# A graph layer on one core: edge tiles of 128 rows in place of 125, another order of SyncE's queue ahead of the mixer, one-hot rows made by pairs

## The reference, cut to what matters

```
xn = layernorm(x)
el, er = (xn W_src + b) . attn_l,  (xn W_dst + b) . attn_r      # 8 heads per node
e      = leaky_relu(el[src] + er[dst]);  a = softmax of e over the edges of one dst
gnn    = segment_sum(feat_v[src] * a, dst)                      # feat_v = xn W_val + b
mix    = linear attention over all nodes (random features of xn Wq, xn Wk; then Wo)
x1     = x + gnn + mix
out    = x1 + expert FFN (8 experts, Sinkhorn gates, top-k rows routed) of layernorm(x1)
```

## Time and profile before

| | us |
|---|---|
| median of 3 runs | 3210.87 (3203.05 to 3212.89) |
| the profiled execution | 3184.74 |
| its span | 3182.6 |
| busy: PE, POOL, DVE, ACT | 2569.4, 2209.5, 1621.1, 993.6 |
| mean granted TensorE clock | 0.907 of full |

### The profile page before, as it was taken

How to read it: one execution, slowest core, us unless ns; L and a number is a source line. 1 busy time by engine, 2 the same in 40 slices (tenths; PEclk the granted TensorE clock), 3 DMA queues, 4 the chain that set the end, 5 groups by cost and what they waited for, 6 DMA issues and landing times.

```text
span 3182.6 us, 47522 instructions
## 1 busy us (share of the span) xinstructions
PE 2569.4 (81%) x10463; PEld 1790.9 (56%) x10464; DVE 1621.1 (51%) x2963; ACT 993.6 (31%) x2564; POOL 2209.5 (69%) x1847
## 2 busy tenths in 40 slices
PE   6689999999999989951676777777888988934998
PEld 3366677776677744420454556665666766723443
DVE  6612222222222269985854555555666666767232
ACT  2312222222222210020454444554555655600111
POOL 6287778777778777877877877777777777600454
PEclk9889999999999989985699998898988999955999
DMA  4341121111111133420566667777777777630111
GB/s 144 122 105 33 31 37 29 29 29 29 30 31 29 23 105 119 117 64 3 157 174 173 176 181 183 185 186 182 194 193 187 196 193 195 175 111 0 45 52 38
DMA packets 276032, 341.23 MB, mean 107 GB/s; under 512 B 164855, under 2 KB 184030, under 8 KB 275850
## 3 DMA queue, kind: packets, MB, share of 16 engines
q0 software_dynamic: 218672, 227.51, 31.6%
q1 hardware_dynamic: 51709, 93.57, 9.1%
q10 hardware_dynamic: 5594, 19.52, 1.7%
HBM read 285.65 MB, written 55.25 MB: 107 GB/s over the span
## 4 chain that ended last, share of the span: by engine, by line
POOL 41%; PE 19%; issue 16%; DMA 13%; DVE 8%; DVEq 2%; POOLq 0%; ACT 0%; ACTq 0%
POOL R L552 31%; PE ps L640 17%; DMA R<-val_tab,src_i 11%; POOL R L594 8%; POOL er_starts L565 2%; DMA work<-in_x_dram 1%; DVEq L239 1%; DVE R L1463 1%; DVE work L1557 1%; DMA R<-in_L_gnn_b_dst_dram 1%; PE ps L934 1%; DVEq L1463 1%; PE ps L664 1%; DVE R L1444 0%; DVE R L1500 0%
## 5 line engine op out<-in xcount | busy, mean ns | idle before, releaser
L640 PE MATMUL ps<-R,work 125*125 (+3 forms) x5240 | 1650.6, 470 | 225.7 <-DVE R L1463 207.2
L640 PEld LDWEIGHTS ps<-R,work 125*125 125x125 f32 (+2 forms) x5240 | 987.6, 195 | 795.0 <-issue 655.7
L552 POOL DMA_INDIRECT R<-el_tab,src_i x800 | 984.6, 1231 | 341.1 <-issue 288.7
L594 POOL DMA_INDIRECT R<-val_tab,src_i x800 | 978.7, 1223 | 280.7 <-issue 180.8
L1463 DVE TENSOR_TENSOR R<-R,ps (+1 forms) x800 | 521.2, 693 | 131.4 <-DVE ps L1452 125.6
L1113 ACT ACTIVATE work<-work 125x125 f32<-125x125 f32 x900 | 277.8, 309 | 500.0 <-PE ps L640 472.1
L640 PE MATMUL ps<-work,R 128*128 128x250 f32 x1600 | 359.5, 383 | 21.8 <-DMA work<-R 21.8
L1110 ACT ACTIVATE work<-work,negdst 125x125 f32<-125x125 f32 x900 | 353.6, 393 | 59.2 <-issue 34.5
L640 PEld LDWEIGHTS ps<-work,R 128*128 128x128 f32 x1600 | 308.9, 194 | 59.1 <-issue 21.8
L1452 DVE COPY ps<-R (+1 forms) x401 | 69.9, 175 | 299.2 <-POOLq L600 227.1
L1295 DVE TENSOR_TENSOR R<-ps,R 125x512 f32<-125x512 f32 x50 | 34.6, 692 | 358.1 <-PE ps L640 358.1
(11 more groups left out here) (256 smaller groups left out, 2186.0 us busy)
## 6 DMA issues: line engine op xcount, KB each, us to landing
work<-in_x_dram SPq DMA_DIRECT2D x33, 500.0 KB
R<-el_tab,src_i POOLq DMA_INDIRECT x800
R<-val_tab,src_i POOLq DMA_INDIRECT x800, 5.9
val_tab<-R SPq DMA_DIRECT2D x50, 253.9 KB
work<-R SPq DMA_DIRECT2D x25, 500.0 KB
work<-xm_tab SPq DMA_DIRECT2D x50, 250.0 KB
out_dram<-R SPq DMA_DIRECT2D x50, 250.0 KB
xm_tab<-work ACTq DMA_DIRECT2D x17, 500.0 KB
```

The costliest lines, as they stand in the source:

```text
L552: eng.indirect_dma_start(out=ELP[:, g, c, :], out_offset=None, in_=el_tab[:, :], in_offset=bass.IndirectOffsetOnAxis(ap=src_i[:, t:t + 1], ...
L594: eng.indirect_dma_start(out=ring[:, slot, :], out_offset=None, in_=val_tab[:, :], in_offset=bass.IndirectOffsetOnAxis(ap=src_i[:, 2 * u + ...
L640: return pe.matmul(o, l, r, start=start, stop=stop)
```

## The change

**Edge tiles.** An edge tile has B = 128 rows. The edges are laid out as 16 chunks of CT = 49 tiles (NT = 784 places), of which NE = 782 hold edges; CL is 6272, and the 13 blocks have 512 columns, the last one 128. `src` and `dst` come from the host as before, 125 to a column. `src` is therefore turned on the chip: ACT loads it, DVE casts it, PE turns it (7 products), DVE copies it (3), SP writes it to DRAM (3 DMAs) and reads it back as 112 rows of 896, PE turns these (7 products), DVE copies them to `src_i` (2). `dst` is loaded as 112 rows of 896, negated by DVE, turned by PE (7 products) and copied by DVE (2), all between mixer and output. The zero fill of `er_starts` and its reading back have 128 rows of partitions in place of 125.

```
+B = 128
+CT = -(-E // (NCH * B))
+CL = CT * B
+NT = NCH * CT
+EQ = NT * B
+NE = -(-E // B)
...
-            for u in range(ET // 2):
+            for u in range(NE // 2):
                 eng.wait_ge(S["tile_free"], 2 * u + 2)
                 gather_pair(u)
...
+            eng.wait_ge(S["consts_ready"], 2)
+            eng.wait_ge(S["edge_rows"], 4)
+            n_ = (NI - 1) * 128 * P
+            eng.dma_start(src_nat[0:n_].rearrange("(j p n) -> p j n", p=128, n=P), src_turned[:, 0:NI - 1, :]).then_inc(S["idx_loaded"], 16)
...
+            eng.wait_ge(S["idx_loaded"], 64)
+            eng.dma_start(src_rows, src_nat.rearrange("(p n) -> p n", p=NR)).then_inc(S["idx_loaded"], 16)
...
+            st.done(v.memset(negdst_rows[lo:NR, REST:NI * B], -NOBODY))
+            st.done(v.tensor_scalar(negdst_rows[lo:NR, 0:REST], dst_i[lo:NR, 0:REST], -1.0, None, ALU.mult))
+            v.tensor_scalar(negdst_rows[0:NR - 1, :], dst_i[0:NR - 1, :], -1.0, None, ALU.mult).then_inc(S["edge_rows"], 1)
+            v.wait_ge(S["edge_psum"], 3)
```

```
             def load_x(g):
                 if g >= NXI:
-                    if g % 2:
-                        return
                     eng.wait_ge(S["xn_transposed"], g - NXI + 1)
...
+                    if g == G - NXI:
+                        load_weights()
```

```
-                for s in range(2):
-                    k2 = 2 * (u + c) + s
-                    fn(absd[s][0:P, :], iota_f[0:P, :], ACT.Abs, bias=negdst[:, bass.ds(2 * u + s, 1)]).then_inc(S["act_step"], 1)
-                    act.wait_ge(S["act_step"], k2 + c + 1)
-                    act.wait_ge(S["onehot_free"], k2 + 1)
+                fn(absd[0], row_of(c), ACT.Abs, bias=negdst[:, bass.ds(2 * u, 1)])
+                fn(absd[1], row_of(c), ACT.Abs, bias=negdst[:, bass.ds(2 * u + 1, 1)]).then_inc(S["act_step"], 1)
+                act.wait_ge(S["act_step"], (u + c) + 1 + shifts)
+                for s in range(2):
+                    act.wait_ge(S["onehot_free"], 2 * (u + c) + s + 1)
```

More of the change, by code:

```diff
@@ L65, in block_tiles @@
 def block_tiles(k):
-    return NCH * (min(TB * k + TB, CT) - TB * k)
+    return sum(c * CT + g < NE for g in range(TB * k, min(TB * k + TB, CT)) for c in range(NCH))
 def logits_by(k):
@@ L385, in store_el, with load_weights @@
                 eng.dma_start(el_v[:, 2 * g:2 * g + 2, :], elr_all[:, 0, 2 * g:2 * g + 2, :]).then_inc(S["el_written"], 16)
[L387 to L396, removed]
+            def load_weights():
                 eng.wait_ge(S["welr_ready"], 1)
@@ L519, in _ @@
             eng.sem_inc(S["consts_ready"], 1)
-            for t_ in (ident[:, :], halves[:, :], half2[:, :], before[:, :], EW2[:, ET // 2, :]):
+            for t_ in (ident[:, :], halves[:, :], half2[:, :], before[:, :]):
                 st.done(eng.memset(t_, 0.0))
@@ L606, in _ @@
                     report(u - BEHIND)
-            for u in range(ET // 2 - BEHIND, ET // 2):
+            for u in range(NE // 2 - BEHIND, NE // 2):
                 report(u)
@@ L998, in trip @@
                     copy_xT(g, b % 2)
-                    if more and b % 2:
-                        load_x(g + NXI, b)
                     if not isinstance(g, int) or g >= 1:
@@ L1237, in fold_logit_weights @@
                 v.wait_ge(S["elr_params"], 96)
-                v.wait_ge(S["rows_spread"], 1)
-                s_al, s_ar, s_bs, s_bd = [ps[:, 4 + r, :] for r in range(4)]
                 for w_, a_, o_ in ((s_wsrc, s_al, 0), (s_wdst, s_ar, H)):
@@ L1387, in _, with columns @@
             v.wait_ge(S["er_t_copied"], NB)
-            def columns(k):
-                return TB * k * P, min(TB * k * P + TB * P, CL)
-            for k in range(NB):
-                lo, hi = columns(k)
-                st.done(v.tensor_tensor_scan(out=scan_x[:, lo:hi], data0=scan_p[:, lo:hi], data1=scan_m[:, lo:hi],
-                                             initial=0.0 if k == 0 else scan_x[:, lo - 1:lo], op0=ALU.mult, op1=ALU.add))
-                st.done(v.tensor_scalar(scan_p[:, lo:hi], scan_p[:, lo:hi], -1.0, -FAR, ALU.add, ALU.mult))
-                st.done(v.tensor_scalar(scan_d[:, lo:hi], scan_d[:, lo:hi], ends[:, 2:3], FAR, ALU.subtract, ALU.mult))
+            st.done(v.tensor_tensor_scan(out=scan_x, data0=scan_p[:, 0:CL], data1=scan_m, initial=0.0, op0=ALU.mult, op1=ALU.add))
+            st.done(v.tensor_scalar(scan_p[:, 0:CL], scan_p[:, 0:CL], -1.0, -FAR, ALU.add, ALU.mult))
             st.done(v.memset(scan_p[:, CL:CL + 1], FAR))
             st.done(v.memset(scan_p[:, 0:1], 0.0))
+            st.done(v.tensor_scalar(scan_d, scan_d, ends[:, 2:3], FAR, ALU.subtract, ALU.mult))
+            def columns(k):
+                return TB * k * B, min(TB * k * B + TB * B, CL)
             for i, k in enumerate(range(NB - 1, -1, -1)):
```

247 lines of the change are left out of this document (150 added, 97 removed).

## The result

The changed kernel takes 4207.88 us in the median of 4 runs (4195.51 to 4217.59), the kernel before 3209.64 (3203.05 to 3212.89): a ratio of 1.3111, with an interval of 1.307 to 1.3153. The forecast was 3015. The profiled execution took 4217.59 us (span 4215.5), against 3184.74 (3182.6) before: 1032.9 us more.

What follows compares the result with a forecast made beforehand. The prediction took the number of POOL's gathers and the price of one to bound the kernel. Its terms, -8 + 1 - 8 - 37 - 144 = -196 us, off a median of 3211 gave 3015 us, range 2955 to 3070.

Steps and rivals of the forecast that it cites:

- The price of a gather: POOL's logit and value gathers: 128 rows cost 1.02 us, with 0.30 between 1.32 us, where 125 rows took 1.51.
- The front: Before the mixer: earlier weights cut PE's idle time, net -8 us, ends -20 and +20.
- The turned dst: Between mixer and output: extra DVE and PE products, PE waits for DVE before the fold, +1 us.
- Scan and logit gathers: Before the message loop: one longer scan saves 8 us; earlier logit gathers remove DVE's 37.5 us wait, -37.
- The loop: Message loop: fewer tiles at POOL's 1.32 us or DVE's time if longer, 1076 us for 1220, -144 us.
- allowance for coupling: Message loop: a loss added for the coupling of POOL and DVE; without it -190 us in place of -144.
- -190: Message loop: the change in us if coupling cost nothing, used for the low end near 2957 us.
- The rest: From the last value gather to the end: the forecast's sum has no term for it.
- The slower rival: Message loop: DMA engines fill up, 1.73 us per tile, loop 1353 us in place of 1257, total 3255 us; chance 0.03.

Runs made afterwards that it cites:

- pad1: Changed kernel with one small GpSimd memset behind each logit gather, all gathers still 128 rows: 2944.5 us on chip 11, 4102.1 us on chip 0.
- l125_v128: Changed kernel with logit gathers of 125 rows, value gathers still 128: 3016.4 us on chip 6, 3332.6 us on chip 5.
- first64: Changed kernel with 128 rows for the first 64 logit gathers and 112 for the other 718: 2944.8 us on chip 11, 4224.1 us on chip 0.
- l64: Changed kernel with logit gathers of 64 rows, value gathers still 128: 2946.2 us on chip 11.

## Why the prediction was wrong

*The price of a gather* was right in kind, and for the mean of a logit gather to the number: 1.02 us taken, 1.018 and 0.963 measured. That number has luck in it: the median is 0.95 for both, and undisturbed gathers are 1.25 us apart, not 1.32; some of the logit gathers take longer.

*The front*: -8 taken, -6.5 measured to PE's start. The turned dst, +1, can't be seen beside the mixer.

*Scan and logit gathers*: -8 and -37 taken, together -45; -53.0 measured for the part between output and value gathers.

*The loop*: -144 taken. On the chips that don't stall it is -201: 1256.7 before, 1055.4 in pad1. Of the 57 us between these, the price has nearly all: 782 gathers at 1.32 in place of 1.25 us are 55. The allowance for coupling was about right: 1257 - 144 = 1113 us are 81 more than 782 x 1.32, and the 1055 measured are 77 more than 782 x 1.25. That -190 was nearer is chance. On the chips that stall it is +103 and the term has the wrong sign.

*The rest* was taken as 0 and is +25; 26 in pad1 as well. With the loop less bound by POOL, more tiles still wait when the last gather is issued: DVE's last pair of products starts 10.9 us after it before (2778.5 and 2767.6), 36.9 us after it in pad1 (2538.0 and 2501.1), and 30.2 us after it in the changed kernel (3805.7 and 3775.5). That is all of pad1's 26 and 19 of the 25.

*The step that failed* is in the first part: "In the mixer and its output the other engines are the last, and the gathers beside them are hidden as long as they end in time." The sum asked of the gathers only when they end. They ended earlier (1352 us against 1506), and on the chips that stall the other engines stood for it: +965.7 us, a term that the sum doesn't have, worth more than all the others together. The profile of before could not show its size, since its long trains of gathers are all of 125 rows; of 112 rows it has 56 gathers and 56 scatters in the tail, each kind 3.8 us apart. That was the moment to write a bound for "what a gather in the new form does to its neighbours", and I bounded only what it costs POOL. The slower rival gave the loop 1353 us and the measured loop is 1360, but that is luck, for its mechanism is another: it said the DMA engines would be full, and their share is 0.60 on a chip that stalls and 0.78 on one that doesn't.

The rule of the Trainium skill on the number of DMA engines (DMA: Bandwidth & Descriptors, "Why a DMA increments its semaphore by 16 and not by 1") divides the runs as the stall does: 5 engines for 125 rows, which no trace shows stalled; 15 for 120 and 16 for 112 and 128. Where it was measured without a stall, a value gather landed in 3.8 us in l125_v128 where it took 5.9 before. The packets from 700 to 1100 us show the spread: a logit gather of 125 rows has 5 packets of 800 bytes and 11 of 100, one of 128 rows 16 of 256. Both have 16 packets of four bytes beside these, as many as the gather raises its semaphore by; so completions do not become more per gather, only more per us, 16 in each 1.25 us and not in 1.51. The rule was used for the gain and not asked for what the spread, or the faster pace that comes with it, might disturb; which of the two does it, no run shows.

Where no stall came, the decomposition of pad1 against the profiled execution of before is -10.8 to the first RECIPROCAL, -1.4, -53.0, -201.3, +26.2: -240.3 us, where -196 was forecast. pad1 leaves nothing out and is the fastest such kernel that ran, 2944.5 us beside 3186.8, 0.924 of it, in one execution of each. On chip 0 it is 1.285 of it. The unedited kernel never ran on a chip without a stall, so what it takes there is not known; its neighbours pad1, first64 and l64 took 2944 to 2946. No version that beats the kernel before on a chip that stalls was found. The nearest candidate is logit and value gathers of 125 rows with the rest of the change. On chip 6 it took 12 us less than 3167, which single executions don't tell from nothing, and it leaves three edges of each tile out.

## What stays open

What the engines wait for. The trace calls it "issue", "remote" and "unknown queue", and names nothing. It is not the bandwidth that the kernel uses, not data of the gather itself (PE stands in the middle of a train of products that need nothing new) and not POOL's time. Whether it is the spread of the rows or the pace is open too, as told above. Why some chips have it and others not, and whether it belongs to the chip or to the occasion, was not settled: six occasions, six chips, four with it (0, 1, 2, 5) and two without (6, 11).

The strongest rival is the recording itself. Each of these executions was recorded to be read, and whether the stall is there in one that nobody records was not tried. The traces give a reason to ask: where there is a stall they lack semaphore updates. first64 on chip 11 has 39303 of them; on chip 0 it has 18310, with as many instructions (47122). l125_v128 has 39299 on chip 6 and 26590 on chip 5, and there even its clean mixer has 3390 landings from 700 to 1100 us in place of 4348. The changed kernel has 555 in that stretch, though its 302 logit gathers alone raise their semaphores by 16 each. So the traces from chips that stall also lack records, and a wait named "issue" or "remote" in such a trace can be one whose end is not recorded. Whether the writing of the records holds the engines up, or both have one cause, no run shows.

## What to carry to other kernels

An operation has two prices, its own time and what it does to the engines beside it. The first can be read off a neighbour in the trace; the second must be measured before a thousand of them are put beside the longest stage. And an experiment proves nothing without the unedited kernel in the same group: two groups of clean runs here pointed to two wrong theories, and only the control on the same chip showed it. A control must also differ in one thing: fewer rows changed the spread and the pace at once.

## What was not expected of the hardware

- Beside indirect gathers of 112, 120 and 128 rows, 1.24 to 1.29 us apart, TensorE and VectorE are held up on some chips, and with them all that waits for these: PE 63 to 71 us busy of 400, against 383 on others. Beside gathers and scatters of 125 rows, 1.5 us apart, no trace shows it (the trace of the kernel before on chip 5, its slowest with 3299 us, was not kept). All of this was seen in recorded executions only.
- One and the same kernel took 2944.8 us on one chip and 4224.1 on another, while the kernel before differed by 5 us between them. Over all six its single runs lay between 3167 and 3299 us.
- 125 rows are the odd case for POOL, as the prediction took it, but it takes no multiple of 16 to be cheap: 64 rows 0.908 us, 112 rows 0.933, 120 rows 0.982, 128 rows 0.947, and 125 rows 1.207 (medians of the logit gathers).
